# Softmax stage of a graph network kernel: GpSimd multiplies three steps of a block instead of two

## The reference

```
w_m = (efeat @ W_msg + b_msg).reshape(E, 16, 16)
w_a = (efeat @ W_attn + b_attn).reshape(E, 16, 16)
h_src = feat[src][:, :, None]
e1 = w_m * h_src
e2 = w_a * h_src
seg_max = segment_max(e2, dst)
ex = exp(e2 - seg_max[dst])
denom = segment_sum(ex, dst)
ft = segment_sum(e1 * ex / denom[dst], dst)
out = ft.sum(axis=1)
```

## Time and profile before

| what | value |
|---|---|
| median of 3 runs | 9570.62 us (9564.91 to 9571.29) |
| profiled execution | 9567.08 us, its span 9565.3 us |
| busy in the span | PE 7830.7 us (82%), DVE 7251.5 (76%), ACT 3104.1 (32%), POOL 7388.2 (77%) |
| granted TensorE clock, mean | 0.907 |
| DMA | 1219.99 MB, mean 128 GB/s |

### The profile page before, as it was taken

How to read it: one execution, slowest core, us unless ns; L and a number is a source line. 1 busy time by engine, 2 the same in 40 slices (tenths; PEclk the granted TensorE clock), 3 DMA queues, 4 the chain that set the end, 5 groups by cost and what they waited for, 6 DMA issues and landing times.

```text
span 9565.3 us, 130175 instructions
## 1 busy us (share of the span) xinstructions
PE 7830.7 (82%) x35619; PEld 4232.1 (44%) x35619; DVE 7251.5 (76%) x13039; ACT 3104.1 (32%) x12664; POOL 7388.2 (77%) x5276
## 2 busy tenths in 40 slices
PE   0799996999974888888888888846998995899994
PEld 0466563555541333333333333313555653455552
DVE  2566662555535999999999999986887885698884
ACT  0111111000004888888888888831000000000000
POOL 5588885788877888888888888846888887588887
PEclk6899996999986999999999999967999997899997
DMA  1344442233323777777777777765323231343332
GB/s 32 96 111 109 111 108 55 61 71 75 65 46 88 210 210 210 210 211 210 211 210 211 210 211 211 211 195 147 84 71 83 71 80 41 98 112 102 102 105 50
DMA packets 819398, 1219.99 MB, mean 128 GB/s; under 512 B 234445, under 2 KB 684119, under 8 KB 798513
## 3 DMA queue, kind: packets, MB, share of 16 engines
q1 hardware_dynamic: 574895, 1003.68, 35.6%
q0 software_dynamic: 208928, 107.90, 9.8%
q10 hardware_dynamic: 35440, 106.85, 3.5%
HBM read 423.03 MB, written 788.86 MB: 127 GB/s over the span
## 4 chain that ended last, share of the span: by engine, by line
POOL 36%; issue 25%; DVE 19%; PE 15%; DMA 2%; DVEq 1%; SPq 1%; ACT 0%; POOLq 0%; ACTq 0%
POOL arena L595 36%; PE PS L1003 10%; DVE arena L1755 6%; DVE arena L1759 4%; DVE arena L1800 3%; PE PS L1027 2%; DVE arena L1776 1%; DVE arena L1766 1%; PE PS L986 1%; DVEq L1747 1%; DVE arena L1933 1%; PE PS L1006 1%; DMA arena<-d_lane 1%; DVE arena L1464 0%; PE PS L1171 0%
## 5 line engine op out<-in xcount | busy, mean ns | idle before, releaser
L1003 PE MATMUL PS<-arena,TB 128*128 128x500 bf16 x16038 | 3577.5, 377 | 189.1 <-DVE TB L1669 176.9
L595 POOL DMA_INDIRECT arena<-d_feat,srci x1650 | 2504.9, 1518 | 554.5 <-issue 434.7
L1003 PEld LDWEIGHTS PS<-arena,TB 128*128 128x128 bf16 x16038 | 1569.8, 100 | 1860.8 <-issue 174.5
L595 POOL DMA_INDIRECT arena<-d_h,srci x1452 | 1910.3, 1316 | 570.8 <-issue 440.2
L825 ACT ACTIVATE arena<-PS,arena 125x32 f32<-125x32 f32 x10560 | 2010.9, 368 | 73.0 <-DMA arena<-d_feat,srci 32.6
L1452 DVE TENSOR_SCALAR arena<-arena,lane 128x1500 bf16<-128x1500 f16 (+1 forms) x1848 | 1246.6, 733 | 580.3 <-DMA arena<-d_lane 354.0
L595 POOL DMA_INDIRECT arena<-d_rel,irel x858 | 1206.8, 1407 | 311.5 <-issue 261.2
L1171 PE MATMUL PS<-arena,ident 125*125 125x512 f32 x1650 | 966.6, 670 | 426.8 <-DVE arena L1759 412.2
L595 POOL DMA_INDIRECT arena<-d_nn,srci x726 | 1037.8, 1429 | 290.7 <-issue 220.4
L1464 DVE SCALAR_TENSOR_TENSOR arena<-arena,lane,PS 128x500 f32<-128x500 f16 x891 | 643.7, 723 | 724.4 <-PE PS L1006 641.1
L1172 PE MATMUL PS<-arena 125*125 125x512 f32 x1650 | 929.1, 647 | 0.0
(11 more groups left out here) (286 smaller groups left out, 7978.5 us busy)
## 6 DMA issues: line engine op xcount, KB each, us to landing
d_smax<-arena SPq DMA_DIRECT2D x165, 1120.0 KB
d_sums_low<-arena SPq DMA_DIRECT2D x330, 560.0 KB
d_sums_high<-arena SPq DMA_DIRECT2D x330, 560.0 KB
arena<-d_pick SPq DMA_DIRECT2D x99, 875.0 KB
arena<-d_lane SPq DMA_DIRECT2D x99, 546.9 KB
d_x<-arena ACTq DMA_DIRECT2D x165, 241.7 KB
arena<-d_x SPq DMA_DIRECT2D x165, 241.7 KB
d_rel<-arena SPq DMA_DIRECT2D x50, 669.4 KB
```

The lines of the kernel that those rows point to most:

```text
L595: gp.indirect_dma_start(out=dst, out_offset=None, in_=table, in_offset=bass.IndirectOffsetOnAxis(ap=index, axis=0)).then_inc(S(sem), 16)
L1003: pe.matmul(PS[:, acc_at(L, q):acc_at(L, q) + w], TB[:, part, g * LANES * F:(g + 1) * LANES * F], OH[L][i][:, g, at:at + w], start=g == 0 ...
```

## The change

A constant `GPN` = 3 takes the place of the 2 in GpSimd's multiply: it now covers steps 7, 8 and 9 of a block (768 elements in one instruction). It waits for the second exponential of the block (steps 6 and 7) instead of the first. VectorE's first `weigh` covers step 6 alone (256 elements in place of 512). The wait of `row_sum` for GpSimd's multiply moves from step 8 to step 7. The number and the order of the instructions of every engine stay as they were.

```diff
+GPN = 3
...
-                gp.wait_ge(S("soft_exp"), 6 * b + 1)
+                gp.wait_ge(S("soft_exp"), 6 * b + 2)
                 if b < NB1 - 1:
                     gp.wait_ge(S("soft_max"), MAXES * (b + 1) + 1)
-                rows = XD[:, s, B1 - 2:B1, :]
-                gp.tensor_tensor(paired(rows, 1), paired(PB[:, s, NA - 2:NA], 1), paired(rows, 0), ALU.mult)\
+                rows = XD[:, s, B1 - GPN:B1, :]
+                gp.tensor_tensor(paired(rows, 1), paired(PB[:, s, NA - GPN:NA], 1), paired(rows, 0), ALU.mult)\
                     .then_inc(S("soft_gp_num"), 1)
...
-                    if t == B1 - 2:
+                    if t == B1 - GPN:
                         dve.wait_ge(S("soft_gp_num"), b + 1)
...
             def late_sums(b, s):
 
-                weigh(b, s, AT, NA - 2)
+                weigh(b, s, AT, NA - GPN)
...
                 top(b, s, 1)
-                weigh(o, z, AT, NA - 2)
+                weigh(o, z, AT, NA - GPN)
                 top(b, s, 2)
```

## The result

| | before | changed |
|---|---|---|
| median | 9564.91 us (9559.06 to 9571.29, 17 runs) | 9590.89 us (9575.72 to 9605.51, 17 runs) |
| ratio, 95% interval | | 1.0027 (1.0019 to 1.0034) |
| first profiled execution | 9567.08 us, span 9565.3, clock 0.907 | 9576.04 us, span 9574.0, clock 0.904 |
| second profiled execution | | 9593.57 us, span 9591.5, clock 0.901 |

The forecast was 9557 us and "about the same". The time lies inside the range on record (9530 to 9606), on the slower side, near the rival "doubled low stretches" (9602).

The account below looks back on a forecast made before the run. VectorE was taken to bound the softmax stage, PE its 1.2 GHz blocks. Saving 0.11 us a block over 155 blocks gave 17 us, less 3 for start and end 14: 9553, by the median's offset 9557 us; range 9530 to 9606.

Parts of the forecast that it names:

- doubled low stretches: Rival, softmax stage: PE's 1.2 GHz periods last 6.83 us, not 3.41, in one block of five; 9602 us; chance 0.25.
- If the pattern settles again, with one block fewer: Softmax stage, likeliest case: full-clock and 1.2 GHz blocks repeat every five, 98.99 us, 19.80 each; 9550 to 9563 us, 0.46.
- low block: Softmax block with PE's clock at 1.2 GHz for a stretch; PE's loop stays at 19.93 us, little or nothing is saved.
- a full block: Softmax block with PE at full clock: shrinks to 19.63 us, moving the next 1.2 GHz stretch by 0.85 us.
- just ahead of the differences: Where a 1.2 GHz stretch began before PE's differences, which follow 2.48 us idling, when it lasted 6.83 us.
- 0.267 us a block from VectorE: VectorE's weigh with 256 elements less gives back 0.267 us; its own loop goes from 19.89 to 19.63 us.
- PE's loop of 19.93 in low blocks: PE from top 10 through six differences to the last sum; stays 19.93 us, VectorE waits 0.3 us at carry.
- 1.93 taken: GpSimd's multiply of 768 elements put at 1.93 us; it ends before top 1 and costs 0 in the settled stage.
- A doubled block: Softmax block with a 6.83 us stretch at 1.2 GHz: 21.29 us long, 1.40 us more.
- The start: First softmax blocks: four multiplies fall outside the products, and one at the end, holding VectorE 3 us together.
- The gather of 3.00 us: One GpSimd gather a block, read as held up by VectorE's sums; to get shorter by 0.6 to 0.9 us.
- The saving arrives in full: Rival: 1.2 GHz stretches move off PE's loop, VectorE's loop decides everywhere; 41 us saved, 9530 us; chance 0.12.

Follow-up runs that it names:

- the run of 9540 us: The profiled, fast run among the first seven of VectorE's part alone: 9540 us, with no doubled block in 150.
- the fills: Constant matmuls in PE's idle time ahead of the differences: changed kernel with ten 9525.49, four 9512.34, two 9535.99 us; kernel before with ten 9559.23, four 9563.90.
- VectorE's part alone: Kernel before, with VectorE's first weigh covering step 6 only, GpSimd keeping two steps and step 7's numerators left out: 9591.41 us, ratio 1.0032.
- two of the four matmuls: Changed kernel with two constant matmuls on PE ahead of the differences, where another run had four (9512.34 us): 9535.99 us, ratio 0.9963.

## Why the prediction was wrong

*The step that failed* is "If the pattern settles again, with one block fewer, the same count gives 5 x 20.48 - 3.41 = 98.99 us for five blocks", taken as the likeliest with 0.46, over doubled stretches with 0.25. What came in its place is the pattern of nine, 180.91 us, with four low and two doubled blocks: 20.10 us a block for the forecast's 19.80, and 26.5 us more in the stage than before for 14 less. The pattern of five exists and has the forecast length. In the first execution, timeline of DVE:

```profile
3554.29 0.69 DVE L1786 TENSOR_TENSOR arena<-PS,arena 125x512 f32<-125x512 f32 x1 [0.23 <-PE PS L1142]
3573.92 0.69 DVE L1786 TENSOR_TENSOR arena<-PS,arena 125x512 f32<-125x512 f32 x1
3593.55 0.68 DVE L1786 TENSOR_TENSOR arena<-PS,arena 125x512 f32<-125x512 f32 x1
...
3653.31 0.69 DVE L1786 TENSOR_TENSOR arena<-PS,arena 125x512 f32<-125x512 f32 x1 [0.22 <-PE PS L1142]
```

These are 99.02 us for five, and it went so from 3158 to 3851. But it didn't last. The fives need the stretch behind the third low block to stay away, and it was due right behind the edge: 1.50 us into the differences at 3759.49, where it stayed away, and 1.48 at 3858.47, where it came. Then a fourth block was low, and the stretches that followed landed ahead of the differences: single at 0.53 us, doubled at 0.70. In the patterns that followed the fourth stretch falls 1.26 to 1.37 us into the differences, well inside the edge, so they hold themselves up; the fives of the run of 9540 us have 1.49 to 1.57. I had seen that a full block now makes a step of 0.85 us and that it "may settle" on the bad place, and gave that too little. No row read before the change favoured one landing over the other, and that should have kept the two chances near each other.

The forecast's windows of the earlier trace rows lie 0.24 us late: the clock falls at 5033.99 and 3777.89, which is why they read 0.52 and 0.54. Its sums use distances alone and stand. But "just ahead of the differences" was 0.58 us (3777.89, the differences at 3778.47), while the series of before opened 0.22 us ahead and did not double.

*What held, with its size:*
- 0.267 us a block from VectorE: 19.90 to 19.63.
- PE's loop of 19.93 in low blocks, with `carry` waiting for it.
- GpSimd's multiply: 1.845 us for 1.93 taken, inside the `product`s, cost nothing in the settled stage.
- A doubled block: 21.27 for 21.29. One in 4.5 (33 of 150) for the rival's one in five; the rival's 9602 stands against 9590.89.

*What did not:*
- The start was to cost 3 us. The twelfth `carry` starts at 3234.93 before, at 3235.02 in the second execution (0.1 us later) and at 3237.29 in the first (2.4).
- The gather of 3.00 us was to get shorter by 0.6 to 0.9. It stayed at 3.02. The time came from all ten: their mean fell from 1,529 ns (its group before) to 1,461, 0.68 us a block.
- "The saving arrives in full" needs no luck with the pattern but PE without the long idling, as the fills show.

*Open:* what moves a block by the hundredths of a us that tip the fives over the edge in most runs, and in one of eight of VectorE's part alone did not. The two edges are read from the traces; no run moved a stretch across one on purpose. What leaves 0.24 us on VectorE in every third block is open too.

## What to carry to other kernels

Here the low stretches of a series began 20.48 us apart, near the length of the kernel's block, and the time was set by how many blocks such a round of n took, n x 20.48 - 3.41 us: five gave 19.80 us a block, six 19.91, nine 20.10. Where the two lengths are so near each other, a saving on another engine moves the count, and may make it worse, though every term of its sum is right. Remove the idling first, with matmuls that nobody reads, and then judge the saving: here it gave 40 us in the stage with them and cost 26 without.

## What I had not expected of the hardware

- The same program on the same chip gave 9540 and 9588 to 9601 us; its mean clock told the two apart, 0.91 and 0.902.
- With two of the four matmuls no stretch doubled any more; four ended the low stretches, with 1.43 us of idling left.
- The places are sharp: 0.56 us ahead of the differences was single and 0.57 doubled, 1.48 us into them was there and 1.49 away, in eight profiles of six kernels.
- One further instruction or wait a block on VectorE came with 0.24 us of idling in every third block, and that with 16 and 17 doubled stretches.
- GpSimd's multiply of two fp32 inputs took 1.29, 1.85 and 2.41 us for 512, 768 and 1,024 elements: 2.2 ns an element and 0.17 us.
